# Routed experts in full and half tiles, and slot arithmetic moved ahead of row maxima, in an attention and mixture-of-experts kernel

## What is computed

```
x = x + attention(xn) + moe(xn)

attention:  q, k, v = split(xn @ w_qkv.T);  softmax(q k^T / sqrt(8)) v;  @ w_proj.T + b_proj
            (one head of 128, all 2048 keys)
moe:        t = xn @ W_in + b_in;  logits = t @ W_gate + b_gate       (8 experts)
            the two best experts of each token, gates = softmax over the two
            eout_e = relu(t @ W1[e] + b1[e]) @ W2[e] + b2[e]          (128 -> 512 -> 128)
            moe = (sum of gate * eout_e) @ W_out + b_out
```

## Time and profile before

| | us |
|---|---|
| median of 3 runs | 242.37 (242.34 to 242.48) |
| the profiled execution | 242.35 |
| its span, first to last instruction | 240.6 |
| PE busy | 226.1 (94%) |
| PE weight loads busy | 214.0 (89%) |
| POOL busy | 140.9 (59%) |
| DVE busy | 136.6 (57%) |
| ACT busy | 111.7 (46%) |

### The profile page before, as it was taken

The page is one execution under the profiler, slowest core; times in us unless marked ns, Lnnn a source line. Parts: engine busy times, 40 slices in busy tenths (PEclk is TensorE's granted clock), DMA queues, the critical chain, the costliest instruction groups (busy, mean ns, idle before and its releaser), DMA issues.

```text
span 240.6 us, 4828 instructions
## 1 busy us (share of the span) xinstructions
PE 226.1 (94%) x1724; PEld 214.0 (89%) x1724; DVE 136.6 (57%) x330; ACT 111.7 (46%) x265; POOL 140.9 (59%) x163
## 2 busy tenths in 40 slices
PE   7699977999999999899999999999899999999983
PEld 7688865889999998899999999999899899999983
DVE  4978585364252551445444445444677886985642
ACT  2572520433524325354444554444656656567561
POOL 3149007888888820266555666553088888888610
PEclk9999999999999999999999999999999999999999
DMA  6799911101111121022222222221111113113201
GB/s 180 282 324 341 322 31 46 45 33 46 46 41 39 43 66 44 14 55 76 70 73 71 67 71 75 69 75 38 33 46 34 44 35 82 40 40 83 75 15 44
DMA packets 23047, 19.54 MB, mean 81 GB/s; under 512 B 3280, under 2 KB 19696, under 8 KB 22768
## 3 DMA queue, kind: packets, MB, share of 16 engines
q1 hardware_dynamic: 20000, 14.71, 20.1%
q0 software_dynamic: 2048, 4.20, 6.5%
q10 hardware_dynamic: 976, 0.33, 0.5%
HBM read 10.97 MB, written 8.26 MB: 80 GB/s over the span
## 4 chain that ended last, share of the span: by engine, by line
PE 78%; DVE 8%; DMA 4%; POOL 3%; issue 2%; ACT 1%; ACTq 1%; POOLq 0%; DVEq 0%
PE ps L1051 15%; PE ps L1037 15%; PE ps L917 10%; PE ps L853 6%; PE ps L792 5%; PE ps L793 5%; PE ps L794 5%; DVE part_max L601 3%; PE ps L926 2%; POOL wtab L380 2%; PE ps L930 2%; PE ps L927 2%; DMA w_raw<-in_L_attn_w_proj_dram 2%; PE ps L1025 2%; PE ps L800 2%
## 5 line engine op out<-in xcount | busy, mean ns | idle before, releaser
L343 POOL COPY wst<-wtab 128x1156 f32 x39 | 45.0, 1154 | 39.3 <-DVE y_sb L738 39.3
L454 ACT ACTIVATE pf<-ps 128x512 f32<-128x512 f32 x64 | 38.1, 595 | 36.5 <-PE ps L794 36.1
L601 DVE TENSOR_REDUCE part_max<-ps 128x1 f32<-128x1024 f32 x32 | 38.9, 1223 | 13.3 <-PE ps L853 13.1
L380 POOL DMA_INDIRECT wtab<-slots_out,slots x32 | 34.4, 1074 | 15.9 <-DMA slots_out<-y_sb 8.4
L353 POOL DMA_INDIRECT slots_in<-hl,slots x32 | 31.5, 985 | 18.7 <-DVE slots L677 11.7
L730 DVE TENSOR_SCALAR mid<-ps,wst 128x128 f32<-128x128 f32 x78 | 23.8, 347 | 32.5 <-PE ps L1037 32.5
L1051 PE MATMUL ps<-wst,mid 128*128 128x128 f32 x312 | 41.3, 275 | 0.7 <-DVE x_sb L628 0.7
L792 PE MATMUL ps<-q_hi,xnT_hi 128*128 128x256 f32 x128 | 41.2, 322 | 0.5 <-ACT q_hi L439 0.5
L1037 PE MATMUL ps<-xgT,wst 128*128 128x128 f32 x312 | 41.3, 275 | 0.0
L1051 PEld LDWEIGHTS ps<-wst,mid 128*128 128x128 f32 x312 | 38.0, 192 | 0.8 <-ACT mid L494 0.8
L1037 PEld LDWEIGHTS ps<-xgT,wst 128*128 128x128 f32 x312 | 38.0, 192 | 0.1
(11 more groups left out here) (145 smaller groups left out, 341.4 us busy)
## 6 DMA issues: line engine op xcount, KB each, us to landing
wtab<-in_L_ffn_W_dram SPq DMA_DIRECT2D x16, 256.0 KB, 5.9
xg<-slots_in SPq DMA_DIRECT2D x39, 64.0 KB, 2.0
slots_out<-y_sb SPq DMA_DIRECT2D x39, 64.0 KB, 1.5
slots_in<-wst SPq DMA_DIRECT2D x2, 1024.0 KB, 5.0
x_sb<-in_L_attn_x_dram SPq DMA_DIRECT2D x4, 256.0 KB, 4.9
out_dram<-x_sb SPq DMA_DIRECT2D x3, 256.0 KB, 2.6
wtab<-in_L_ffn_b_dram SPq DMA_DIRECT2D x1, 512.0 KB, 7.4
slots_in<-hl,slots POOLq DMA_INDIRECT x32
```

Source lines behind the costliest of these rows:

```text
L343: pool.tensor_copy(wst[:, t % 4, :], wtab[:, bass.ds(experts[t], 1), :].rearrange("p a n -> p (a n)")).then_inc(Z["staged"], 1)
L380: pool.indirect_dma_start(out=z[:, j, c, :], out_offset=None, in_=slots_out, in_offset=bass.IndirectOffsetOnAxis(ap=slots[:, c, j:j + 1], ...
L454: act.activation(pf[:, i % 3, :], ps[:, st_bank(i), :], ACT.Exp).then_inc(Z["pf_done"], 1)
L601: dve.tensor_reduce(part_max[:, g % 2, m // 2, m % 2:m % 2 + 1], ps[:, b:b + 2, :], AX.XY, ALU.max).then_inc(Z["max_read"], 1)
```

## The change

Tiles. The 4096 rows fill 32 full tiles (`NF`). An expert's rest of 1 to 64 rows goes to a half tile of 64 rows, a rest of 65 to 127 to a full tile; 7 half tiles (`NU`) are reserved, two to a "double" tile (`ND = 4`, the last with one half). The doubles stand at turns 8, 16, 24 and 32 of 36. The ring of staged weights has 6 places. In a double tile each half has its own expert: layer 1 in 64 columns per half; layer 2 with W2 stationary and 64 columns of `mid` streamed, so the result is transposed; ACT copies it to `cT`, and PE transposes it back one turn later.

Routing. `route_slots` is replaced by three parts, which stand on DVE's queue at step 3 of group 0, ahead of the step's maxima and of those that follow; they also work out where half tiles lie. `route_experts` compares twice. The first pair of group 1 moves from step 4 to step 2.

The diff, cut to its core:

```diff
-    MT = (TOPK * S + NE * (SL - 1)) // SL
-    MS = MT + 1
+    HU = SL // 2
+    NF = TOPK * S // SL
+    NU = (TOPK * S + NE * (HU - 1)) // HU - 2 * NF
+    ND = (NU + 1) // 2
+    MT = NF + ND
+    MS = NF + 2 * ND
+    DOUBLE_AT = [8, 16, 24, 32]
+    RING = 6
-    PAIR_STEP = [[4, 5, 5, 6]] + 6 * [[1, 2, 4, 5]] + [[]]
+    PAIR_STEP = [[2, 4, 5, 6]] + 6 * [[1, 2, 4, 5]] + [[]]
...
-            def stage(t):
-                if t >= 4:
-                    pool.wait_ge(Z["y_ready"], t - 3)
-                pool.tensor_copy(wst[:, t % 4, :], wtab[:, bass.ds(experts[t], 1), :].rearrange("p a n -> p (a n)")
+            def stage(n):
+                t = TILE_OF[n]
+                at = ORDER[t] if HALVES[t] == 0 else NF + 2 * (ORDER[t] - NF) + n - ENTRY[t]
+                if n == ENTRY[t]:
+                    if HALVES[t]:
+                        load_experts(at, HALVES[t])
+                    elif ORDER[t] % 8 == 0:
+                        load_experts(at, 8)
+                if n >= RING:
+                    pool.wait_ge(Z["y_ready"], TILE_OF[n - RING] + 1)
+                pool.tensor_copy(wst[:, n % RING, :], wtab[:, bass.ds(experts[at], 1), :].rearrange("p a n -> p (a n)")
...
+            def yT_copy(t):
+                act.wait_ge(Z["yT_done"], 1 + ORDER[t] - NF)
+                act.activation(yT_at(t), ps[:, MA, 0:HU * HALVES[t]], ACT.Copy).then_inc(Z["yT_copied"], 1)
...
+            def route_slots_a():
                 link("route", dve.tensor_copy(tot[every], total.rearrange("p j e -> p e j")))
                 link("route", dve.tensor_tensor_scan(cum[every].rearrange(flat), first_tile[every].rearrange(flat),
                                                      tot[every].rearrange(flat), 0.0, ALU.mult, ALU.add))
                 link("route", dve.tensor_tensor(over[every], cum[:, :, NT - 1:NT].to_broadcast([P, NE, NT]),
                                                 thr[:, :].unsqueeze(1).to_broadcast([P, NE, NT]), ALU.is_gt))
+                link("route", dve.tensor_reduce(tiles_e[:, :], over[every], AX.X, ALU.add))
+                link("route", dve.scalar_tensor_tensor(out=left_e[:, :], in0=tiles_e[:, :], scalar=-float(SL),
+                                                       in1=cum[:, :, NT - 1], op0=ALU.mult, op1=ALU.add))
                 dve.tensor_tensor(cum[every], cum[every], tot[every], ALU.subtract)
+                dve.tensor_tensor_scan(tiles_c[:, :], ones[:, 0:NE], tiles_e[:, :], 0.0, ALU.mult, ALU.add)
+                link("route", dve.tensor_scalar(halves_e[:, :], left_e[:, :], 0.0, None, ALU.is_gt))
+                dve.tensor_tensor(tiles_x[:, :], tiles_c[:, :], tiles_e[:, :], ALU.subtract)
+                dve.tensor_scalar(full_end[:, :], tiles_c[:, :], float(SL), None, ALU.mult)
+                link("route", dve.tensor_tensor_scan(halves_c[:, :], ones[:, 0:NE], halves_e[:, :], 0.0, ALU.mult, ALU.add))
                 link("route", dve.scalar_tensor_tensor(out=cum[every], in0=tiles_x[:, :].unsqueeze(2).to_broadcast([P, NE, NT]),
                                                        scalar=float(SL), in1=cum[every], op0=ALU.mult, op1=ALU.add))
+            def route_slots_b():
+                link("route", dve.tensor_tensor(shift[:, :], halves_c[:, :], halves_e[:, :], ALU.subtract))
+                link("route", dve.scalar_tensor_tensor(out=shift[:, :], in0=shift[:, :], scalar=-float(HU), in1=full_end[:, :],
+                                                       op0=ALU.mult, op1=ALU.subtract))
+                link("route", dve.tensor_scalar(shift[:, :], shift[:, :], float(HU * (2 * NF + NU - 1)), None, ALU.add))
+                dve.tensor_tensor(lg[every], below(), cum[every].rearrange("p e j -> p j e"), ALU.add).then_inc(Z["prefix_read"], 1)
                 dve.wait_ge(Z["prefix_read"], 1)
+                link("route", dve.tensor_tensor(eq[every], lg[every], full_end[:, :].unsqueeze(1).to_broadcast([P, NT, NE]), ALU.is_ge))
+                link("route", dve.tensor_tensor(eq[every], eq[every], shift[:, :].unsqueeze(1).to_broadcast([P, NT, NE]), ALU.mult))
+                link("route", dve.tensor_tensor(lg[every], lg[every], eq[every], ALU.add))
+            def route_slots_c():
...
             def route_experts():
+                no_less(tile_no, tiles_c, texp_f)
+                no_less(half_no, halves_c, texp_h)
+                link("route", dve.tensor_tensor(texp_h[:, :], texp_h[:, :], texp_f[:, :], ALU.subtract))
+                link("route", dve.tensor_scalar(texp_b[:, :], texp_f[:, :], float(NE), None, ALU.is_ge))
+                link("route", dve.tensor_tensor(texp_h[:, :], texp_h[:, :], texp_b[:, :], ALU.mult))
+                link("route", dve.tensor_tensor(texp_f[:, :], texp_f[:, :], texp_h[:, :], ALU.add))
...
             for g in range(PRE):
                 for k in range(STEPS[g]):
+                    if g == 0 and k == 3:
+                        route_slots_a()
+                        route_slots_b()
+                        route_slots_c()
                     for m in pairs_at(g, k):
                         pair_max(g + 1, m)
...
-                    if g == 0 and k == 3:
-                        route_slots()
...
             def layer1(t):
+                    for n, w, rows in parts(t):
+                        for c in (2 * h, 2 * h + 1):
+                            at = SL * (c % 2) + w
+                            last = pe.matmul(ps[:, 2 * (t % 2) + h, at:at + rows.stop - rows.start],
+                                             wst[:, n % RING, P * c:P * (c + 1)], xgT[:, t % 2, rows], start=True, stop=True)
...
+            def layer2_halves(t):
+                for n, _, rows in parts(t):
+                    for c in range(HC):
+                        last = pe.matmul(ps[:, MA, rows], wst[:, n % RING, DM + D * c:DM + D * (c + 1)], mid[:, t % 2, c, rows],
+                                         start=(c == 0), stop=(c == HC - 1))
+                last.then_inc(Z["yT_done"], 1)
+            def turn_halves(t):
+                pe.wait_ge(Z["yT_copied"], 1 + ORDER[t] - NF)
+                pe.wait_ge(Z["y_ready"], t - 1)
+                pe.transpose(ps[0:HU * HALVES[t], y_bank(t), 0:D], yT_at(t), ident[:, 0:P]).then_inc(Z["y_done"], 1)
...
-                layer2(t)
+                if t >= 1 and HALVES[t - 1]:
+                    turn_halves(t - 1)
+                if HALVES[t]:
+                    layer2_halves(t)
+                else:
+                    layer2(t)
```

More of the change, by code:

```diff
@@ L27, in attention_moe_kernel @@
     SL = P
-    MT = (TOPK * S + NE * (SL - 1)) // SL
-    MS = MT + 1
+    HU = SL // 2
[5 more added lines that the diff above has]
+    DOUBLE_AT = [8, 16, 24, 32]
+    ORDER = []
+    for _t in range(MT):
+        ORDER.append(NF + DOUBLE_AT.index(_t) if _t in DOUBLE_AT else _t - sum(d < _t for d in DOUBLE_AT))
+    HALVES = [0 if n < NF else min(2, NU - 2 * (n - NF)) for n in ORDER]
+    RING = 6
+    ENTRY = [sum(max(1, HALVES[q]) for q in range(_t)) for _t in range(MT + 1)]
+    TILE_OF = [max(_t for _t in range(MT) if ENTRY[_t] <= n) for n in range(ENTRY[MT])]
+    NW = ENTRY[MT]
     ER = 2 * DM + D + HC
@@ L99, in attention_moe_kernel @@
         hl = sb("hl", [P, NT, HW])
-        q_hi = sb("q_hi", [P, 2, BK], FP32R)
-        q_lo = sb("q_lo", [P, 2, BK], FP32R)
+        q_hi = sb("q_hi", [P, 2, max(SIZE)], FP32R)
+        q_lo = sb("q_lo", [P, 2, max(SIZE)], FP32R)
         pf = sb("pf", [P, 3, BK])
@@ L160, in attention_moe_kernel @@
         tiles_x = sb("tiles_x", [P, NE])
+        left_e = sb("left_e", [P, NE])
+        halves_e = sb("halves_e", [P, NE])
+        halves_c = sb("halves_c", [P, NE])
+        full_end = sb("full_end", [P, NE])
+        shift = sb("shift", [P, NE])
         tile_no = sb("tile_no", [P, MS])
+        half_no = sb("half_no", [P, MS])
         cmp = sb("cmp", [P, MS, NE])
         texp_f = sb("texp_f", [P, MS])
+        texp_h = sb("texp_h", [P, MS])
+        texp_b = sb("texp_b", [P, MS])
         texp = sb("texp", [P, MS], I32)
@@ L216, in hl_banks, with parts, yT_at @@
             return ps[:, b:b + 2, 0:2 * HW].rearrange("p b (j n) -> p b j n", n=HW)
+        def parts(t):
+            if HALVES[t] == 0:
+                return [(ENTRY[t], 0, slice(0, SL))]
+            return [(ENTRY[t] + h, HU * h, slice(HU * h, HU * (h + 1))) for h in range(HALVES[t])]
+        def yT_at(t):
+            d = ORDER[t] - NF
+            return cT[:, SL * d:SL * d + HU * HALVES[t]]
         def y_bank(t):
@@ L361, in _ @@
                         pool.wait_ge(Z["wT_copied"], 5)
-                        load_experts(0, 8)
                     stage(STAGE_AT.index(n))
-            for t in range(4, MT):
-                if t % 8 == 0:
-                    load_experts(t, min(8, MS - t))
-                stage(t)
-            pool.wait_ge(Z["staged"], MT)
+            for n in range(len(STAGE_AT), NW):
+                stage(n)
+            pool.wait_ge(Z["staged"], NW)
```

(26 more changed lines are left out.)

59 lines of the change are left out of this document (35 added, 24 removed).

## The result

| | before | after |
|---|---|---|
| median, us | 242.36 (242.29 to 242.48, 4 runs) | 248.5 (246.51 to 248.81, 4 runs) |
| the profiled execution, us | 242.35 | 248.75 |
| its span, us | 240.6 | 247.0 |
| its mean granted clock | 0.998 | 0.976 |

The changed kernel takes 1.0236 times as long (95% interval 1.0181 to 1.029), so it is slower. The direction was forecast; the size wasn't: 245.1 was predicted with a range up to 247.1. Of its four runs three have a mean granted clock of 0.976 to 0.978 and take 248.3 to 248.8 us; the fourth has 0.990 and takes 246.5 us.

The account below looks back on a forecast made before the run. TensorE (PE), 94% busy, was taken to bound the kernel, through its own work and its idle moments. 242.37 + 0.60 (slot arithmetic) + 2.15 (experts' numbers) + 0 (expert stage) = 245.1 us, range 244.3 to 247.1.

Parts of the forecast that it names:

- Part 1, the expert stage: PE's expert stage: 663 records become 664, the 64-column ones still 0.111 us each, so the time changes by zero.
- The choice was between 0.056 and 0.111 us: Cost of a 64-column record in the expert stage; 0.111 us taken, 0.056 a rival at 238.9 us, chance 0.07.
- the two rules: Skill page on matmul cost: load time follows weight columns (107 ns for 128), against about 60 cycles at 1 to 64 streamed columns.
- The new wait and the relus: Double tiles: PE's wait for ACT's copy covered by 0.4 us, DVE's relu two tiles on by 0.5 us.
- Part 2: Slot arithmetic ahead of group 1's maxima on DVE: slots 2.64 us later, row maximum and PE's work behind it 0.60 us later.
- Part 3: Experts' numbers at step 0 of group 1: 2.15 us added on DVE before a maximum PE awaits, all reaching PE.
- a sign of being wrong: The prediction counts as wrong if, among other signs, the clock row shows 0.5 near 40 us.
- a rival, for the first wait: Clock falls around PE's 4.1 us idle before group 1's third pair, costing 1.5 us: 246.5 us, chance 0.28.
- the forecast 0.57: Chance given to the main forecast of 245.1 us, with the clock at 1.00 from 34 to 45 us.
- The second wait: PE idle 2.2 us before the second pair of group 2; no clock fall was priced for it.
- The 3 us: Length of running at half clock, read from the run's first 28 records; half of it lost, 1.5 us.

Follow-up runs that it names:

- experiment 8: The kernel before with five streams of 20 fp32 products appended, differing in weight and streamed columns; 261.6 us, a time without meaning.
- experiment 4: The changed kernel with the experts' numbers at step 6 of group 1 and 17 dummy products in TensorE's wait before group 1's third pair; 242.8 us, ratio 1.0019.
- experiment 1: The changed kernel with 17 dummy products ahead of the third pair of group 1 and 9 ahead of the second pair of group 2; 245.0 us, ratio 1.0123.
- experiment 3: The changed kernel with the experts' numbers at step 6 of group 1 instead of step 0, no dummy products; 243.67 us, ratio 1.0056.
- experiment 5: The kernel before, 39 full tiles, with only the routing side: first pair at step 2, slot arithmetic moved, spare operations for the added ones; 248.21 us, ratio 1.0238.
- experiment 2: The changed kernel with 17 dummy products ahead of the third pair of group 1 only, none ahead of group 2's second pair; 245.52 us, ratio 1.015.
- experiment 6: The kernel before with the first pair of group 1 at step 2 and slot arithmetic ahead of the second maximum, nothing lengthened; 241.19 us, ratio 0.9963.

## Why the prediction was wrong

**Part 1, the expert stage: right.** 664 records, a 64-column record at 0.11 us, a stage of 72.9 against 73.1 us. The choice was between 0.056 and 0.111 us, and the row of 136 streamed columns pointed to a floor. Experiment 8 shows that the floor is the weight load, and experiment 4 that the stage is worth nothing in time: its profiled span is 0.5 us longer than before (241.1 against 240.6), and 0.38 and 0.22 us of delay were there before the experts began. The Trainium skill, "TensorE: Matmul & The Clock Gate", section "LDWEIGHTS (loading the stationary operand)", has the load's time follow its columns alone, and 0.11 us at 128 columns and 0.06 at 64 agree. The table of its section "Back-to-back issue gap" (about 60 cycles up to 64 streamed columns) is for products without a budget for the load, as the section says itself; so the two rules don't part ways, as the prediction had it. Here, where each product loads weights of its own, the trace has 0.11 us at 32 streamed columns.

**The new wait and the relus: right.** The timeline of ACT's copy of the turned result and of PE's transposing it back:

```profile
123.06 0.28 ACT L548 ACTIVATE cT<-ps 128x128 f32<-128x128 f32 x1 [1.55 <-PE ps L1154]
...
123.87 0.27 PE L1161 MATMUL ps<-ident,cT 128*128 128x128 f32 x1
```

The copy ended at 123.34, 0.5 us before PE needed it (0.4 forecast), and PE wasn't idle ahead of it.

**Part 2: right as arithmetic.** The maximum behind `slots` was due 2.64 us later than 34.98; it is at 37.46, 2.5 later. With the clock held, the row maximum's transposes come at 43.05 against 42.59: 0.46 for the 0.60 forecast.

**Part 3: right.** From `cmp` to the maximum 3.67 us (49.31 to 52.98), where 3.59 was worked out; PE's mark moved by 2.2.

The sum of these, 245.1, is what experiment 1 measures when PE doesn't idle: 245.0.

**What failed is the clock: the sum has no term for it.** The forecast took the granted clock as 1.00 from 34 to 45 us; it was 0.50 from 37.4 to 44.1, which the prediction had named as a sign of being wrong, and again from 54.5 to 57.7. The two falls cost 2.25 and 1.7 us; 3.4 us lie between 245.1 and the measured 248.5. I had the clock only as a rival, for the first wait, with a chance of 0.28 and a price of 1.5 us, and that was off in three places.
- The chance. None of the twelve runs that have the wait of 4.1 us unfilled (the changed kernel's, experiments 3 and 5) has a mean clock above 0.991, where the kernel before has 0.996 to 1.000; three of them were profiled, and all three show the fall. The prediction had said that the length of the wait speaks for it, and still gave the forecast 0.57. What it put against it, that it depends on where the stretch falls, shows in these runs in when the clock fell, not in whether.
- The second wait. It had no rival and no term. 2.26 us is enough, at times: in the changed kernel the fall after it cost 1.7 us, in experiment 5 it came after 2.41 us, and in experiment 2 it came in some runs and not in others. This is the larger omission: with the first fall alone the sum is 246.6 at the price of 1.5, inside the range, and 247.35 at what it cost, just outside.
- The price. 1.5 us was right for a fall that begins when PE is back at work: 1.45 in experiment 3, 1.7 for the second fall of the changed kernel. But the first fall of the changed kernel put 5.4 us of PE's work at the lower level, not 3, and cost 2.25. Why it lasted longer there is open. The 3 us came from the distance of records at the start of the run, a weak source: the granted clock in the rows of 1.5 to 4.0 us reads 1.00, although only 13 records stand in these 2.5 us, where 23 would at 0.11 us.

With the falls measured here (2.25 and 1.7) the sum is 249.0; the median is 248.5. In the profiled execution the arithmetic on DVE brought 0.46 and 2.23 us, and the falls of the clock around the two waits 3.95: what followed the stillness was dearer than the delay that caused it.

## What to carry to other kernels

Before narrowing the streamed side of a product, look at whether its weight load is as long: with 128-column weights a record of 64 columns cost the same 0.11 us, and only both halved gave 0.06. Price a new wait of TensorE of two microseconds or more with a fall of the clock behind it (1.45 to 2.25 us here, by a mark of the queue right behind it; in every run at 4.1 us, in some at 2.05 to 2.4), and price every such wait, not only the longest. Where the wait can't be moved, fill it with products that nobody reads: 26 of them made this kernel 3.5 us faster. Bookkeeping on another engine costs nothing or everything depending on whose release stands behind it in the queue: the same experts' numbers cost 2.2 us (experiments 1 and 4, the clock held) to 4.8 us (the changed kernel and experiment 3) at step 0, and next to nothing at step 6 (242.8 us in experiment 4 is within 0.6 of the kernel before).

## What the runs showed of the hardware

- With a wait of 4.06 to 4.16 us left unfilled the granted clock went to 0.50 in all three profiled runs: once 2.7 us into the wait, for 6.7 us (the changed kernel), twice about a microsecond after PE had started again, for 3.4 us (experiments 3 and 5). After 2.26 and 2.41 us it fell in the profiled runs of the changed kernel and experiment 5; after 2.2 and 2.05 us it didn't in those of experiments 2 and 6. At 0.50 the four records of 256 columns took 1.91 us instead of 1.03.
- The clock can fall with PE at work without a break: at about 257.5 us of experiment 8, among fp32 products of 128 weight columns and 32 streamed columns.
- The changed kernel spread by 2.3 us (246.51 to 248.81) where the kernel before, in four runs beside it, spread by 0.2 (0.65 in thirteen later ones); its run at 246.51 has a mean clock of 0.990, the others 0.976 to 0.978. Not all spread is the clock's: experiment 4 spreads by 1.0 us at 0.996 to 1.000.
- Taking ten vector additions out from between indirect scatters on POOL, to speed them up, let ACT and DVE wait for up to 6 us at a time and TensorE for up to 4.2, and cost 11.6 us against the same kernel with the additions left in (254.69 and 243.06). Why is open.
